# Carrying 32x32-block transposes through DRAM in a gated cross-attention and feed-forward block

## The reference

```python
def attention(query, mem):                       # query (4,1024,256), mem (4,154,256)
    q, k, v = query @ Wq.T + bq, mem @ Wk.T + bk, mem @ Wv.T + bv
    scores = einsum('btd,bsd->bts', q, k) / sqrt(256)
    vals, idx = top_k(scores, 32)                # all other scores become -inf
    attn = softmax(masked scores)
    return einsum('bts,bsd->btd', attn, v) @ Wo.T + bo

def ffn(h):                                      # 256 -> 1024 -> 256
    return relu(h @ W1 + b1) @ W2 + b2

x = x + tanh(g_xattn) * attention(layernorm(x), ctx)
x = x + tanh(g_ffn) * ffn(layernorm(x))
```

## Time and profile before

| | us |
|---|---|
| median of 3 runs | 255.32 |
| lowest, highest | 255.27, 256.47 |
| span of the profiled execution | 254.5 |
| PE busy in it | 249.7 |
| DVE, POOL, ACT busy | 177.6, 171.4, 152.4 |

### The profile page before, as it was taken

How to read it: one execution, slowest core, us unless ns; L and a number is a source line. 1 busy time by engine, 2 the same in 40 slices (tenths; PEclk the granted TensorE clock), 3 DMA queues, 4 the chain that set the end, 5 groups by cost and what they waited for, 6 DMA issues and landing times.

```text
span 254.5 us, 6003 instructions
## 1 busy us (share of the span) xinstructions
PE 249.7 (98%) x2014; PEld 242.8 (95%) x2014; DVE 177.6 (70%) x744; ACT 152.4 (60%) x388; POOL 171.4 (67%) x264
## 2 busy tenths in 40 slices
PE   8999999999999999999999999999999999999995
PEld 7866898999999999999999999999999999999994
DVE  2798999999996398588757794679448795421042
ACT  2576677865664755575466565675566657555652
POOL 3457996897995893569636993669456964696300
PEclk9999999999999999999999999999999999999999
DMA  7992203103312210321120211001100001001011
GB/s 223 379 416 117 66 18 107 27 3 93 115 43 85 82 43 35 91 84 45 41 85 9 76 43 45 0 3 43 43 3 0 10 34 45 1 29 56 0 44 41
DMA packets 6878, 17.30 MB, mean 68 GB/s; under 512 B 800, under 2 KB 2368, under 8 KB 6592
## 3 DMA queue, kind: packets, MB, share of 16 engines
q1 hardware_dynamic: 6848, 16.93, 19.0%
HBM read 12.44 MB, written 4.19 MB: 65 GB/s over the span
## 4 chain that ended last, share of the span: by engine, by line
PE 90%; DVE 6%; POOL 2%; issue 1%; ACT 0%; POOLq 0%; ACTq 0%
PE y_ps L435 11%; PE y_ps L431 11%; PE z_ps L418 11%; PE z_ps L420 11%; PE y_ps L430 11%; PE z_ps L419 11%; PE sc_ps L345 6%; PE pt_ps L366 2%; PE att_ps L400 1%; PE att_ps L387 1%; DVE left L960 1%; PE att_ps L384 1%; PE att_ps L386 1%; PE y_ps L247 1%; PE att_ps L385 1%; DVE top L956 1%
## 5 line engine op out<-in xcount | busy, mean ns | idle before, releaser
L1279 POOL TENSOR_TENSOR hid_lo<-hid,hid_hi 128x256 fp32r<-128x256 f32 x120 | 87.0, 744 | 34.6 <-ACT hid L748 33.9
L747 ACT ACTIVATE hid_hi<-z_ps,small_in 128x256 fp32r<-128x256 f32 x128 | 60.6, 473 | 70.1 <-PE z_ps L420 69.8
L418 PE MATMUL z_ps<-x2nt_hi,w_hi 128*128 128x256 f32 x256 | 73.1, 285 | 0.0
L420 PE MATMUL z_ps<-x2nt_hi,w_lo 128*128 128x256 f32 x256 | 71.5, 279 | 0.0
L419 PE MATMUL z_ps<-x2nt_lo,w_hi 128*128 128x256 f32 x256 | 71.1, 278 | 0.0
L430 PE MATMUL y_ps<-w_hi,hid_hi 128*128 128x256 f32 x248 | 66.0, 288 | 0.0
L431 PE MATMUL y_ps<-w_lo,hid_hi 128*128 128x256 f32 x248 | 64.5, 282 | 0.0
L748 ACT ACTIVATE hid<-z_ps,small_in 128x256 f32<-128x256 f32 x128 | 60.4, 472 | 0.0
L435 PE MATMUL y_ps<-w_hi,hid_lo 128*128 128x256 f32 x248 | 50.4, 282 | 0.0
L418 PEld LDWEIGHTS z_ps<-x2nt_hi,w_hi 128*128 128x128 f32 x256 | 48.3, 188 | 0.0
L419 PEld LDWEIGHTS z_ps<-x2nt_lo,w_hi 128*128 128x128 f32 x256 | 48.2, 188 | 0.0
(11 more groups left out here) (155 smaller groups left out, 404.2 us busy)
## 6 DMA issues: line engine op xcount, KB each, us to landing
x_ring<-x SPq DMA_DIRECT2D x8, 512.0 KB, 4.5
out<-x SPq DMA_DIRECT2D x15, 256.0 KB, 2.0
xt_in<-x_t SPq DMA_DIRECT2D x7, 512.0 KB, 3.6
w_in<-w SPq DMA_DIRECT2D x2, 1024.0 KB, 10.8
wkq_in<-w_kq SPq DMA_DIRECT2D x1, 514.0 KB, 3.4
wvo_in<-w_vo SPq DMA_DIRECT2D x1, 513.0 KB, 6.6
xt_in<-x_t SPq DMA_DIRECT2D x2, 256.0 KB, 4.9
ctx_in<-ctx_t SPq DMA_DIRECT2D x1, 462.0 KB, 10.1
```

Of the source, the lines that this page charges most:

```text
L418: mm(dst, w1_hi[:, k, cols], hi[:, k, toks], start=k == 0, stop=False)
L420: last = mm(dst, w1_lo[:, k, cols], hi[:, k, toks], start=False, stop=k == KD - 1)
L747: func(hid_hi[:, c % RING, :], z_ps[c % 2][:, 0:2 * P], ACT.Relu, bias=b1[:, c:c + 1]).then_inc(hid_hi_made, 1)
L1279: nc.gpsimd.tensor_tensor(hid_lo[:, slot, :], hid[:, slot, :], hid_hi[:, slot, :], ALU.subtract).then_inc(hid_lo_made, 1)
```

## The change

Group 0 is transposed by PE as before. From the second group on (`FIRST_MOVED = 1`, groups 1 to 7) PE transposes nothing. DVE transposes each 32x32 block where it lies (`block_picked`, two instructions; `block_x2n`, one), which leaves a block of the result in the partition quarter that its rows came from. SP then issues four stores, one per partition quarter, each of which puts four 32x128 pieces (64 KB) into the places in a DRAM tensor where they belong, waits until all four have landed, and issues one load of 256 KB, which brings the transposed operand back into SBUF with the rows in the right partitions (`picked_t`, `x2n_t`). ACT and DVE make the hi and lo parts out of these tiles in SBUF instead of out of PSUM. The repetition of the 26 rest rows, which ACT made with `copy_rest`, is a broadcast in the second block transpose, so `copy_rest` stays for group 0 alone.

```diff
+        picked_rows = nc.dram_tensor("picked_rows", (GROUPS, 2, P, 4 * P), f32, kind="Internal").ap()
...
+            sums = pt_ps if a >= FIRST_MOVED and p == 1 else att_ps
...
+        def by_block(rows, r):
+            return rows[:, r * 4 * BLOCK:(r + 1) * 4 * BLOCK].rearrange("(q i) c -> i q c", i=BLOCK)
+        def in_tokens(v):
+            return v.rearrange("p k (t q i) -> p q (k t) i", q=BLOCKS, i=BLOCK)
...
+            def store_picked(a, p):
+                n = a - FIRST_MOVED
+                sp.wait_ge(picked_blocked, 2 * (2 * n + p + 1))
+                for q in range(BLOCKS):
+                    sp.dma_start(by_block(picked_rows[a, p], q), picked_blocks[q * BLOCK:(q + 1) * BLOCK, p, :, :]).then_inc(picked_stored[p], 16)
+            def move_picked(a, p):
+                n = a - FIRST_MOVED
+                sp.wait_ge(picked_stored[p], 16 * BLOCKS * (n + 1))
+                if a > 0:
+                    sp.wait_ge(pt_lo_made, 4 * (a - 1) + 2 * p + 2)
+                sp.dma_start(picked_t[:, p, :, :].rearrange("p q c -> p (q c)"), picked_rows[a, p]).then_inc(picked_moved[p], 16)
...
+            store_picked(4, 1)
+            move_picked(4, 1)
+            load_xt(7)
+            store(2, 1)
+            store_x2n(4, 0)
+            move_x2n(4, 0)
+            store_picked(5, 0)
...
-                func(x2nt_hi[a % 2][:, :, 2 * p * P:2 * (p + 1) * P], xn_ps[p][:].rearrange("p (k c) -> p k c", k=KD),
-                     ACT.Copy).then_inc(x2nt_hi_made, 1)
+                    func(in_tokens(hi), in_runs(x2n_t[:, p, :, :]), ACT.Copy).then_inc(x2nt_hi_made, 1)
...
+                    main, rest = in_tokens(pt_hi[:, 0:1, :]), in_tokens(pt_hi[32:64, 1:2, :])
+                    moved = picked_t[:, p, :, :]
+                    nc.vector.tensor_tensor(in_tokens(pt_lo[:].rearrange("p (k c) -> p k c", k=1)),
+                                            in_runs(moved[:, :, 0:2 * BLOCK]), main, ALU.subtract).then_inc(pt_lo_made, 1)
+                    nc.vector.tensor_tensor(rest, in_runs(moved[32:64, :, 2 * BLOCK:4 * BLOCK]), rest, ALU.subtract).then_inc(pt_lo_made, 1)
...
+                nc.vector.transpose(out[:, :, 0, :, :], main).then_inc(picked_blocked, 1)
+                nc.vector.transpose(out[:, 0:BLOCKS - 1, 1, :, :], rest).then_inc(picked_blocked, 1)
...
+                nc.vector.transpose(x2n_blocks[:, p, :, :].rearrange("p r (k t i) -> p (r k) t i", t=2, i=BLOCK), pair).then_inc(x2n_blocked, 1)
...
-        hid = sb("hid", [P, RING, 2 * P])
+        hid = w1_in[:].rearrange("p k (s n) -> p (k s) n", n=2 * P)
```

More of the change, by code:

```diff
@@ new lines, in _ @@
+            ffn_in(4, 7)
+            attend(3, 0)
+            ffn_out(4, 3)
+            scores(5, 0)
+            ffn_out(4, 4)
+            ffn_out(4, 5)
+            ffn_out(4, 6)
+            ffn_in(5, 0)
+            ffn_in(5, 1)
+            ffn_out(4, 7)
+            ffn_in(5, 2)
+            ffn_in(5, 3)
+            ffn_out(5, 0)
+            ffn_in(5, 4)
+            ffn_in(5, 5)
+            scores(5, 1)
+            ffn_in(5, 6)
+            attend(3, 1)
+            ffn_out(5, 1)
@@ new lines, in _ @@
+            ffn_out(5, 2)
+            ffn_out(5, 3)
+            ffn_in(5, 7)
+            ffn_out(5, 4)
+            ffn_out(5, 5)
+            ffn_in(6, 0)
+            ffn_out(5, 6)
+            ffn_in(6, 1)
+            ffn_in(6, 2)
+            scores(6, 0)
+            ffn_in(6, 3)
+            ffn_out(5, 7)
+            ffn_in(6, 4)
+            ffn_in(6, 5)
+            ffn_out(6, 0)
+            ffn_out(6, 1)
+            ffn_in(6, 6)
+            ffn_in(6, 7)
+            ffn_out(6, 2)
@@ new lines, in _ @@
+            ffn_out(6, 3)
+            attend(4, 0)
+            ffn_out(6, 4)
+            ffn_out(6, 5)
+            ffn_in(7, 0)
+            ffn_in(7, 1)
+            ffn_out(6, 6)
+            ffn_in(7, 2)
+            scores(6, 1)
+            ffn_in(7, 3)
+            ffn_out(6, 7)
+            ffn_out(7, 0)
+            ffn_out(7, 1)
+            ffn_out(7, 2)
+            ffn_in(7, 4)
+            attend(4, 1)
+            ffn_in(7, 5)
+            ffn_in(7, 6)
+            ffn_out(7, 3)
@@ new lines, in _ @@
+            scores(7, 0)
+            ffn_in(7, 7)
+            ffn_in(8, 0)
+            ffn_out(7, 4)
+            ffn_in(8, 1)
+            ffn_out(7, 5)
+            ffn_out(7, 6)
+            ffn_in(8, 2)
+            ffn_out(7, 7)
+            ffn_out(8, 0)
+            ffn_in(8, 3)
+            ffn_in(8, 4)
+            scores(7, 1)
+            ffn_in(8, 5)
+            ffn_in(8, 6)
+            attend(5, 0)
+            ffn_out(8, 1)
+            ffn_in(8, 7)
+            ffn_out(8, 2)
@@ L640, in _ @@
+            ffn_in(15, 7)
+            ffn_out(15, 1)
+            ffn_out(15, 2)
+            ffn_out(15, 3)
+            ffn_out(15, 4)
+            ffn_out(15, 5)
             last_ffn_out()
@@ new lines, in _ @@
+            pt_to_lo(6, 1)
+            scale_scores(7, 1)
+            topk_round(7, 1, 0)
+            pick(7, 0)
+            block_picked(7, 0)
+            output(5, 0)
+            residual(6, 1)
+            topk_round(7, 1, 1)
+            x2nt_to_lo(6, 0)
+            block_x2n(6, 1)
+            topk_round(7, 1, 2)
+            topk_round(7, 1, 3)
+            pick(7, 1)
+            block_picked(7, 1)
+            pt_to_lo(7, 0)
+            output(5, 1)
+            x2nt_to_lo(6, 1)
@@ L1159, in _ @@
             last_hid_to_lo(2)
[L1160 to L1162 removed]
+            output(7, 0)
+            last_hid_to_lo(3)
+            last_hid_to_lo(4)
+            last_hid_to_lo(5)
+            last_hid_to_lo(6)
+            last_hid_to_lo(7)
             last_output(0)
```

1167 lines of the change are left out of this document (811 added, 356 removed).

## The result

The changed kernel takes 258.2 us (median of four runs, 257.7 to 261.3) against 255.4 us for the kernel before in the same comparison: ratio 1.011, 95% interval 1.007 to 1.015. The forecast was 247.2 us, so it had the wrong sign and missed by 11 us. The profiled execution took 258.5 us, with a span of 256.7 us, 1.8 less; the forecast's 0.8 us set the median of the runs against the span of one execution.

The account below looks back on a forecast made before the run. The prediction took TensorE (PE) to bound the kernel: 254.5 - 12.3 for removed transposes + 4.2 for uncovered VectorE waits = 246.4 us of span, forecast as 247.2 us with the 0.8 us to the runs' median; range 242.3 to 253.0 us.

Parts of the forecast that it names:

- the forecast's 0.8 us: Added to the predicted span because the median of the runs, 255.3 us, lay that far over the profiled span.
- TensorE's 12.3 us: Groups 1 to 7: 28 transpose quads of 0.44 us leave TensorE's list, all taken off the time.
- Block transposes at 1.4 us per half: VectorE, groups 1 to 7: three added block transposes per half group, 2.8 us per group.
- rival (d): VectorE becomes the bound, with transposes at 2.3 us per half and dearer port waits: 266 us, slower; chance 0.10.
- Port, 0.7 us per half: VectorE: three subtractions per half with both operands in SBUF take turns with POOL, 0.23 us each, 1.4 us per group.
- The first 42 us at 0, bounds of 1: Start of the kernel: reordering wins or loses nothing of TensorE's 2.0 us idle there, bounds -1 and +1 us.
- VectorE's budget, 0.6 us of uncovered wait per group, 4.2 us in all: Groups 1 to 7: VectorE's 24.4 us of work against TensorE's 26.44 leaves few waits uncovered; bounds 0 and 28 us.
- The move at 6.2 us: Four stores and a load through DRAM per half and kind, covered by TensorE's other work, 13.7 of 15.2 us; cost 0.
- (e): Rival: losses of TensorE waits eat the 12.3 us and the time stays, 255 us; chance 0.06.
- (c): Rival: moves are late, SP's waits meeting on half of the 28 moves, 8.4 us more, 251.4 us; chance 0.14.

Follow-up runs that it names:

- e4: Changed kernel with block transposes mostly left out, no DRAM stores or load back, and subtractions reading PSUM: 247.4 us, ratio 0.970 to the kernel before.
- e3: Changed kernel with the three subtractions per half reading a PSUM bank instead of SBUF from the third group on (values wrong): 253.7 us, ratio 0.991 to the kernel before.
- e6: Changed kernel with group 0's first normalised-row subtraction ahead of a pick pair, TensorE's and ScalarE's lists following: 260.4 us, ratio 1.018 to the kernel before.
- e2: Changed kernel without the DRAM stores and load back, block-transposed tiles read as they lie in SBUF: 254.5 us, ratio 0.997 to the kernel before.
- e9: Changed kernel with one out store ahead of two moves on SyncE's list, each load right behind its stores: 255.0 us, ratio 0.996 to the kernel before.
- e7: Changed kernel with rest columns split on VectorE right behind the pick, replacing a later 32-partition subtraction: 259.6 us, ratio 1.014 to the kernel before.

## Why the prediction was wrong

**TensorE's 12.3 us: right.** e4 shows 12.5. But the sum had no term for what a wait costs beyond its idle time. PE is busy for 242.0 us in the changed kernel, 4.8 more than in e4. About 1.7 us of it (0.06 of 28.2) is the lower clock behind the stall at 162 to 170 us. The rest would be matmuls that start anew after a wait and stand alone (0.39 us behind a wait, as in the two rows of TensorE above) where they otherwise overlap; this part is argued from the rows, not tried by itself. The clock does not make the loss: the one run of the changed kernel with a mean granted clock of 1.000 took 257.7 us.

**Block transposes at 1.4 us per half: right.** 442 + 336 + 708 ns = 1.49 us. The 2.3 us of rival (d) was worked out from a figure that the Trainium skill (VectorE: DVE Perf Modes, "The three transpose paths") gives for bf16, and these operands are float32; the measured sum is two thirds of it.

**Port, 0.7 us per half: right in size.** (635 - 420) + (732 - 417) + (763 - 679) = 614 ns. The forecast left out the pick itself, whose mean rose from 546 to 624 ns. e3 shows the cause, and that it was worth 5.2 us of time rather than being one small entry in a budget.

**The first 42 us at 0, bounds of 1: wrong, first failing step.** TensorE idles 1.6 us more there than before, and another 2.5 us from 42 to 62 us, where it had none; 3.5 of these 4.1 us stay in e4. I had read the new order there for its instructions and not followed its waits: TensorE stands for 1.7 us before the second quad of picked probabilities, whose bank is freed by a subtraction that VectorE has behind two picks of 2.15 us. e6 shortened the idle time by 0.8 us and gained no time, so what the start alone is worth is not shown.

**VectorE's budget, 0.6 us of uncovered wait per group, 4.2 us in all: wrong, second failing step.** I put 24.4 us of work against 26.4 from one stretch of the kernel before. The work was about as much as forecast, but the new order brings the top-k rounds forward, so that it lies at 27.1, 27.0 and 26.3 us of 28.2 up to 147 us and at 15.9 after 203: an average hid a peak. TensorE's idle time from 62 to 231 us is 5.9 us, and with it go the 4.6 us of PE time above 237.4: 10.5 us instead of 4.2. That is near the 10.4 us that e4 gives back when transposes, way and port are cut together.

**The move at 6.2 us: right where nothing stands between; hidden by 1.5 us and costed at 0: wrong, third failing step.** Stores issued 1.8 us, wait 1.3, load 2.9 to 3.4: 6.0 to 6.5 us. In the stretch shown above it took 9.8 us (151.35 to 161.13), since the next half's stores and the out store stood ahead of the load. e2 shows that the way cost 3.7 us of the 10.4 when taken out alone, and e9 got 3.8 us back by the order of the queue alone. I had looked at what stands behind a waiting load, the next half's stores, and not at the out stores in the same list, which landed after 3.2 us instead of 2.0 and which VectorE waits for two groups later.

Together: 4.1 at the start, 5.9 - 4.2 = 1.7 of idle later, and 242.0 - 237.4 = 4.6 of PE time make the 10.4 us between 246.4 and 256.7 us of span. Of the rivals, (e) came nearest, losses of TensorE's waits that eat the 12.3 us, at a chance of 0.06; they ate some 15. (c) named the queue but the wrong victim, and (d) the right engine, but no such price was needed: VectorE was 95% busy and not over 100. That the order of its list decides, and not the amount of work alone, is argued from e2, where it is 98% busy from 118 to 147 us and TensorE does not wait. A chance of 0.10 for slower was too small with five engines' lists rewritten at once.

## What to carry to other kernels

Work moved off the bounding engine onto in-order queues must be budgeted by stretch and not by group average, and followed by the oldest buffer that each queue frees: here the one repair that gained 3.8 us was to put a store of finished output ahead of two moves. Compare an operand's old and new home as carefully as the operation. When every list is tight, one local repair mostly hands the wait to the next list, so cut each cost away first to learn what it is worth.

## What the runs showed of the hardware that I had not expected

A block transpose of 32 elements per partition still takes 0.17 to 0.21 us on VectorE, against 0.71 us for 512. Copies and subtractions of 64 to 128 elements per partition with all operands in SBUF (e7) took 0.41 to 0.44 us on average, as much as one of 256 elements with an operand in PSUM (0.42), but their median is 0.23 us and the longest took 1.2 us: a mean can hide a wait. A 256 KB store landed after 3.2 us in the changed kernel and after 2.0 us in the one before, where the moves (32.0 against 17.3 MB of traffic) were not beside it. And 3.3 us of idle on TensorE within 8 us were followed by 4 us at a granted clock of 0.66, so this stall was paid for again right after it. It is not a matter of idle time alone: e9's execution had a granted clock of 0.96 over its first 42 us with 3.1 us of idle, the changed kernel's 1.00 with 3.6.
